# GNN and mixture-of-experts layer: node normalisation and gate logits moved into the closing visits of the attention stage

## The chip, the cores and the metric

The kernel runs on one core of a Trainium2 chip. The metric is device time of one execution in microseconds (us). A core has five engines with instruction streams of their own: TensorE (PE; its weight loads are listed as PEld), VectorE (DVE), ScalarE (ACT), GpSimd (POOL) and SyncE (SP). They meet only at semaphores, and 16 DMA engines serve all of them. "SPq", "POOLq" and the like are the queues that issue an engine's instructions.

## The reference

There are 6250 nodes with 256 features and 206,250 edges sorted by target node. The computation, cut to what matters:

```
h   = layernorm(x)                          # 6250 x 256
z   = h @ W                                 # 4 heads of 64
es, ed = (z * a_src).sum(-1), (z * a_dst).sum(-1)
e   = leaky_relu(es[src] + ed[dst])         # per edge and head
out = segment_sum(softmax_per_dst(e) * z[src], dst)
x   = x + out
hn  = layernorm(x)
logits = hn @ gate_w + gate_b               # 16 experts, the top 2 are taken
y   = hn + moe(hn)                          # 2 of 16 experts, hidden size 512
x   = x + layernorm(y) * gamma + beta
```

## The kernel before

Nodes stand in 49 tiles of 128. The program has five stages with a barrier of all engines between them: A (projection to z), B (attention), C (normalise, gate, sort the tokens to experts), D (experts), E (combine and store). The change touches B and C, and one load of A.

Stage B works in visits. 128 x 4 edges are a group, there are 403 groups, and a visit is one pair of a group and a tile of target nodes that the group touches: 403 - 1 + 49 = 451 visits, in order, written out without a loop (`written_out`, L90). A pass over all visits stands in a loop that runs once with these inputs. In step i each engine does, in the order in which its list stands (L776, L829, L861), the stages whose lag fits:

- POOL gathers the 512 rows of z of a group with four indirect DMAs into a slot of `ring` (L629 to L639). Before group g it waits until the messages of group g - 4 are made (`group_free`, `LEAD` = 4), although the ring has eight slots.
- SP relays each landed group to ACT (L580) and loads the target numbers of two groups at a time into `dst_bc`.
- ACT copies the source terms `es_edge` of visit i - 8 (L807), writes the target numbers of visit i - 9 (L796) and takes the exponent of visit i - 9 (L814, L816).
- DVE makes the one-hot matrix `ST` of visit i (L688), the argument of the exponent of visit i - 6 in four small steps (L702, L707, L713, and the clamp L720, which signals `b_arg`), adds visit i - 9 to the sums `acc` (L775), makes the one-hot `S` (L694) and the weighted messages (L761) of visit i - 7.
- PE multiplies `ST` of visit i with the node terms into `psE` (`destination`, L847) and then `S` with the messages of visit i - 7 into `psM` (`weigh`, L858).

`S`, `ST` and `msg` have eight buffers each (`SR`), and `S` and `ST` lie in the memory of `xs`, on top of 32 tiles of x. The results of two visits share a bank of `psE`: before an even visit v, `destination` waits for the clamp of visit v - 7, and `e_add` waits until both visits of its bank are written.

The number of a tile's last visit depends on the input, but tile t is surely closed after visit 402 + t. So work on closed tiles can be written only beside the last visits. Before, `settle` and `weight` (L729, L818) scale the sums of the first 36 tiles there, and add and take the statistics of the first 12. The pass ends with SP waiting for every semaphore, clearing 24 of them one by one (L620 to L622) and releasing the engines; a barrier follows, in which POOL drains.

Stage C then reloads x over `S` and `ST` (L923 to L925), scales the last 13 tiles on ACT (L979), and in a pipeline over 49 tiles adds the sums to x (L1105), takes statistics (L1062), inverts the deviation, normalises a tile (L1128), stores it to `norm_rows` for stage D (L932), transposes it on PE (L1008), copies it on ACT (L977), multiplies it with the gate (L1016) and keeps 16 logits per node (L1134). After the last logit, top-2 and the sorting of tokens begin on DVE (L1143). Beside this POOL makes an iota and masks (L939 to L946), and DVE some constants (`setup`, L1070), which wait for POOL only at the tenth tile.

Of the kernel before, what the change touches and what calls it, by code (L numbers as in the profile page):

```python
# [28 lines left out]
I32 = mybir.dt.int32  # L29
# [5 lines left out]
P = 128  # L35
G = 4
RING = 8
LEAD = 4
# [12 lines left out]
AHEAD = 6  # L51
ZR = 12
# [37 lines left out]
def written_out(count, unroll, stages):  # L90

    for i in range(count + max(lag for _, lag in stages)):
        for stage, lag in stages:
            v = i - lag
            if 0 <= v < count:
                stage(v, v % unroll, v // unroll)
# [7 lines left out]
def gnn_moe_kernel(nc, E, x, x_turned, src_cols, dst_cols, dst_flat, dst_last, W, a_src, a_dst, gate_w, gate_b, w1, b1, w2, b2, gamma, beta, out):  # L104
# [18 lines left out]
    KEPT = NT - 1 - 32  # L123
# [25 lines left out]
    with whole:  # L149
# [17 lines left out]
        acc = sb(attention, "acc", [P, NT, ROW])  # L167
        esed = sb(attention, "esed", [P, NT, 2 * HEADS])
# [7 lines left out]
        group_free = sb(graph, "group_free", [1, GROUPS + RING - LEAD], I32)  # L176
# [46 lines left out]
        with ExitStack() as ctx:  # L223
# [28 lines left out]
            def _(sp):  # L252
# [120 lines left out]
            def _(dve):  # L373
# [71 lines left out]
                def aside(t, s, r):  # L445
# [18 lines left out]
                    if t == TABLES + 6:  # L464
# [12 lines left out]
                        step(nc.vector.tensor_tensor(group_free[:, RING - 1:GROUPS + RING - LEAD], psA[2][0:1, 0:GROUPS - LEAD + 1],  # L477
                                                     iota_f[0:1, 0:GROUPS - LEAD + 1], ALU.add))
# [14 lines left out]
                dve.wait_ge(a_late, 16 * 3)  # L493
# [38 lines left out]
        b_vstep = sem("b_vstep")  # L532
        b_pstep = sem("b_pstep"); b_nodes = sem("b_nodes")
        b_landed = [sem(f"b_landed{i}") for i in range(RING)]
        b_group = sem("b_group"); 
        PAIRED, PAIRS = RING // 2, -(-GROUPS // 2)
        b_dst = [sem(f"b_dst{i}") for i in range(PAIRED)]; b_rows = sem("b_rows"); b_over = sem("b_over"); b_go = sem("b_go")
# [5 lines left out]
        SETTLED = 3 * PART  # L543
        CLOSED = VISITS - 1 - (NT - SETTLED)
        assert CLOSED >= 0 and CLOSED + 11 >= 2 * 8 + (VISITS - 2 * 8) // 8 * 8
        SH = 2 * HEADS
        PASS_STEPS = 8
        FIN_STEPS = 2 + BULK - 1
        SR = 8
        with ExitStack() as ctx:  # L550
# [5 lines left out]
            stats_b = decided[:, :, :].rearrange("p t h -> p (t h)")[:, 0:PART * 6].rearrange("p (t c) -> p t c", c=6)  # L556
# [4 lines left out]
            dst_bc = sb(ctx, "dst_bc", [P, RING, G * P], BF16)  # L561
            earg = sb(ctx, "earg", [P, 4, 3, G * HEADS])
            msg = sb(ctx, "msg", [P, SR, G, ROW])
            psE = [ps(ctx, f"psEb{i}") for i in range(SR // 2)]
            psM = [ps(ctx, f"psMb{i}") for i in range(2)]
            psP = [ps(ctx, f"psPb{i}") for i in range(2)]

            def dest_of(s):

                return psE[s // 2][:, (s % 2) * G * SH:(s % 2 + 1) * G * SH]  # L570
# [3 lines left out]
            def _(sp):  # L574
                npass = sp.value_load(npass_i[0:1, 0:1], min_val=1, max_val=PASSES_MAX)
                with sp.Fori(0, npass) as k:
# [12 lines left out]
                    def replace_pair(g, at):  # L589

                        done = sp.value_load(group_free[0:1, bass.ds(g + 1, 1)], min_val=1, max_val=VISITS)
# [11 lines left out]
                    for g in range(GROUPS):  # L603
# [4 lines left out]
                        if g % 2 and g // 2 + PAIRED < PAIRS:  # L608
                            replace_pair(g + RING - 1, g // 2 % PAIRED)
# [3 lines left out]
                    for done, total in ((b_group, GROUPS), (b_rows, PAIRS), (b_S, VISITS), (b_ST, VISITS), (b_dest, VISITS), (b_estep, 3 * VISITS),  # L613
                                        (b_arg, VISITS), (b_p, VISITS), (b_msg, VISITS + 1), (b_sum, VISITS), (b_acc, VISITS), (b_es, VISITS),
                                        (b_fstep, FIN_STEPS), (b_rden, 1), (b_scaled, SETTLED), (b_added, PART // BATCH), (b_stats, PART),
                                        (b_var, 1), (b_pstep, PASS_STEPS), (b_nodes, 1)):
# [918 lines left out]
```

## Time and profile before

| | |
|---|---|
| Median of 3 runs | 2792.49 us (2790.86 to 2793.21) |
| The profiled execution, own time | 2791.16 us |
| Its span | 2789.3 us |
| Busy share: PE, DVE, ACT, POOL | 81%, 61%, 24%, 66% |
| Mean granted TensorE clock | 0.821 |
| Stage A | 0 to 78 us |
| Stage B | 78 to 2147.7 us |
| Stage C | 2147.7 to 2300.6 us, its tile pipeline until 2228.9 us |
| Stages D and E | from 2300.6 us |

Times of rows count from the span's start. An engine that is busy all the time is not always the one that sets the pace: here the idle time before each instruction, and what ended it, tell more than the shares. A row of the timeline merges consecutive instructions of one group and gives their start, the time that they took together, and in brackets the idle time before them with its releaser. "issue" means that the engine waited for nothing that the profile shows. The granted clock is 0.5 at 1.2 GHz and 1.0 at 2.4 GHz.

### The profile page before, as it was taken

To read this page: it belongs to the slowest core of one execution; us is meant where nothing else is said; L and a number is where in the kernel's file an instruction comes from. 1 tells how busy PE (TensorE), PEld (TensorE's weight loads), DVE (VectorE), ACT (ScalarE), POOL (GpSimd) and SP (SyncE) were. 2 spreads that over 40 slices of the span, in tenths; PEclk is the share of its full clock that TensorE was granted. 3 is DMA by queue.
4 is the path that set the end of the run, shared out by engine and by line. 5 is a ranking of instruction groups with operands and counts; after the bars stand their busy time and mean duration, and the time that the engine had idled before them with its cause. 6 is when DMAs were issued, how large, how long until landed. Compare 5 with 4: busy or idle time off the path is not lost. (4 is left out here: it accounts for less than half of the span.)

```text
span 2789.3 us, 54969 instructions
## 1 busy us (share of the span) xinstructions
PE 2258.7 (81%) x10829; PEld 1890.7 (68%) x10830; DVE 1711.3 (61%) x4828; ACT 682.4 (24%) x2857; POOL 1849.1 (66%) x1949
## 2 busy tenths in 40 slices
PE   7688787877878788887888888777884848999997
PEld 5576666666666666666766666666663818999985
DVE  6666666666666666666666666666666674333336
ACT  4111111111111111111111111111115415555557
POOL 0677777777777777777777777777774025555547
PEclk9677888788787887888787788888877559999998
DMA  9444444445454444555454554444554207633328
GB/s 315 121 133 133 130 133 131 133 133 132 132 133 133 133 132 130 133 133 133 133 134 134 133 133 133 132 128 133 134 132 127 87 0 243 197 103 106 107 93 278
DMA packets 183503, 382.70 MB, mean 137 GB/s; under 512 B 38837, under 2 KB 86880, under 8 KB 182474
## 3 DMA queue, kind: packets, MB, share of 16 engines
q0 software_dynamic: 87744, 243.02, 32.6%
q1 hardware_dynamic: 79656, 122.51, 13.7%
q10 hardware_dynamic: 15842, 14.43, 2.0%
q8 instruction: 74, 1.21, 0.2%
q14 instruction: 187, 1.53, 0.2%
HBM read 345.87 MB, written 33.93 MB: 136 GB/s over the span
## 5 line engine op out<-in xcount | busy, mean ns | idle before, releaser
L636 POOL DMA_INDIRECT ring<-z_table,src_idx x1612 | 1556.4, 965 | 496.0 <-issue 458.1
L858 PE MATMUL psMb<-msg,xs 128*128 128x260 f32 x3608 | 1202.5, 491 | 255.4 <-DVE msg L761 253.5
L858 PEld LDWEIGHTS psMb<-msg,xs 128*128 128x128 f32 x3608 | 827.1, 241 | 432.4 <-DVE msg L761 284.0
L847 PEld LDWEIGHTS psEb<-nodes,xs 128*128 128x128 f32 x3608 | 550.0, 224 | 269.3 <-issue 238.2
L847 PE MATMUL psEb<-nodes,xs 128*128 x3608 | 522.7, 272 | 156.5 <-DVE xs L688 155.9
L761 DVE TENSOR_TENSOR msg<-ring,psPb 128x1024 f32<-128x1024 f32 x451 | 546.4, 1211 | 0.0
L807 ACT COPY es_edge<-ring 128x16 f32 x451 | 91.8, 204 | 1679.2 <-SPq L583 1642.6
L702 DVE TENSOR_TENSOR earg<-es_edge,psEb 128x16 f32<-128x16 f32 x451 | 76.1, 169 | 559.5 <-ACT es_edge L807 555.4
L694 DVE TENSOR_TENSOR xs<-iota_f,psPb 128x512 f32<-128x512 f32 x451 | 305.9, 678 | 0.1
L688 DVE TENSOR_SCALAR xs<-dst_bc,iota_p 128x512 f32 x451 | 229.9, 510 | 99.5 <-issue 95.2
L1275 POOL DMA_INDIRECT rows_sb<-norm_rows,src_sb x108 | 109.8, 1017 | 168.1 <-DVE src_sb L1352 149.7
L1307 PE MATMUL psHd<-xT,w_sb 128*128 128x128 f32 x1728 | 213.2, 277 | 0.0
L775 DVE TENSOR_TENSOR acc<-acc,psMb 128x260 f32 x451 | 188.1, 417 | 36.8 <-PE psMb L858 31.4
L1319 PE MATMUL psYd<-w_all,hid 128*128 x864 | 204.4, 380 | 0.3 <-ACT hid L1342 0.3
L1307 PEld LDWEIGHTS psHd<-xT,w_sb 128*128 128x128 f32 x1728 | 204.2, 194 | 0.1
L1363 DVE COPY xT<-psXd 128x256 f32<-128x256 f32 x108 | 45.9, 425 | 255.9 <-PE psXd L1297 255.9
L1319 PEld LDWEIGHTS psYd<-w_all,hid 128*128 128x128 f32 x864 | 156.1, 191 | 17.3 <-issue 0.5
L1330 ACT COPY w_sb<-w_all 128x1024 f32 x108 | 112.8, 1045 | 156.7 <-PE psHd L1307 96.6
L1282 POOL DMA_INDIRECT pair_rows<-y_sb,dst_sb x108 | 107.0, 991 | 45.5 <-issue 36.1
L1342 ACT ACTIVATE hid<-psHd,b1T 128x128 f32<-128x128 f32 x432 | 123.6, 368 | 34.1 <-issue 25.9
L796 ACT ACTIVATE psPb<-dst_col,visit_base 128x4 f32 x451 | 120.5, 267 | 1.4 <-issue 1.4
L814 ACT ACTIVATE msg<-earg 128x16 f32<-128x16 f32 x451 | 91.0, 202 | 54.2 <-DVE earg L720 49.5
(209 smaller groups left out, 1413.3 us busy)
## 6 DMA issues: line engine op xcount, KB each, us to landing
dst_bc<-dst_rows SPq DMA_DIRECT2D x202, 256.0 KB, 3.5
ring<-z_table,src_idx POOLq DMA_INDIRECT x1612
w_all<-in_L_ffn_w_dram SPq DMA_DIRECT2D x32, 512.0 KB
b_sb<-in_L_ffn_b_dram ACTq DMA_DIRECT2D x108, 128.0 KB, 3.1
got<-pair_rows SPq DMA_DIRECT2D x48, 256.0 KB, 4.2
xs<-in_x_dram SPq DMA_DIRECT2D x5, 1536.0 KB, 10.9
z_table<-z_out SPq DMA_DIRECT2D x49, 130.0 KB, 6.3
norm_rows<-xnc SPq DMA_DIRECT2D x49, 128.0 KB, 1.7
```

The costliest lines, as they stand in the source:

```text
L636: nc.gpsimd.indirect_dma_start(ring[:, s, c, :], None, z_table, bass.IndirectOffsetOnAxis(ap=at, axis=0)).then_inc(b_landed[s], 16)
L688: nc.vector.tensor_scalar(ST[:, s, :], dst_bc[:, bass.ds(slot, 1), :].rearrange("p o f -> p (o f)"), iota_p[:, 0:1], None, ALU.is_equal).t ...
L694: nc.vector.tensor_tensor(S[:, s, :, :], over(iota_f[:, 0:P].unsqueeze(1), [P, G, P]), over(psP[s % 2][:, G * HEADS:G * HEADS + G].unsquee ...
L761: nc.vector.tensor_tensor(msg[:, s, :, 0:D].rearrange("p g (h d) -> p g h d", h=HEADS), ring[:, bass.ds(slot, 1), :, 0:D].rearrange("p o g ...
L775: nc.vector.tensor_tensor(at, at, psM[s % 2][:, 0:ROW], ALU.add).then_inc(b_acc, 1)
L796: nc.scalar.activation(psP[s % 2][:, G * HEADS:G * HEADS + G], dst_col[:, bass.ds(group * G, G)], ACT.Identity, bias=visit_base[:, v:v + 1])
L847: last = nc.tensor.matmul(dest_of(s)[:, c * SH:(c + 1) * SH], ST[:, s, c * P:(c + 1) * P], nodes[:, bass.ds(tile, 1), :].rearrange("p o c ...
L858: last = nc.tensor.matmul(psM[s % 2][:, 0:ROW], S[:, s, c, :], msg[:, s, c, :], start=c == 0, stop=c == G - 1)
L1307: last = nc.tensor.matmul(psH[s % 2][:, f * P:(f + 1) * P], w1_sb[:, s % 2, c, f * P:(f + 1) * P], xT[:, s % 2, c, :], start=c == 0, stop= ...
L1319: last = nc.tensor.matmul(psY[s % 2][:, 0:D], hid[:, s % 2, f, :], w2_f, start=f == 0, stop=f == FC - 1)
L1330: nc.scalar.copy(w1_sb[:, s % 2, :, :].rearrange("p c f -> p (c f)"), w_all[:, bass.ds(e, 1), 0:KD * F].rearrange("p o f -> p (o f)")).the ...
L1342: last = nc.scalar.activation(hid[:, s % 2, f, :], psH[s % 2][:, f * P:(f + 1) * P], ACT.Relu, bias=b1T[:, bass.ds(e, 1), f:f + 1].rearran ...
```

## The change

Four things change together.

- Memory: `S` and `ST` become tensors of their own, so x stays in `xs`, and the reload in stage C goes. The ring falls from eight groups to four, with the same wait for group g - 4; `dst_bc` keeps eight (`ROWS`). `S`, `ST` and `msg` have four buffers (`MR`) instead of eight.
- Banks: four visits share one bank of `psE` (`BANKED` = 4), which leaves two banks for `psT` and `psL`. Before a visit v divisible by four, `destination` waits for the clamp of visit v - 5, which DVE makes in step v + 1; `e_add` waits until all four visits of its bank are written.
- The work: `finish` on DVE, ACT and PE takes over the whole per-tile pipeline of stage C. In batches of three tiles the denominators are inverted (DVE), the sums scaled (ACT), added to x and measured (DVE). Each six tiles the root is taken (ACT, between two exponents) and inverted. From step 426 on one tile per step is normalised (now on ACT), stored (issued by ACT), transposed (PE), copied (ACT), multiplied with the gate (PE) and its logits kept (DVE). `psT` and `psL` are single. The last batch is tiles 45 to 48; tile 48 is normalised in step 474, and the visits end in step 459. Stage C begins with the constants, a wait for POOL's iota and mask, and top-2.
- The turn of a pass: 35 semaphores with consecutive numbers are cleared by one instruction, and POOL drains right after its last gather.

```diff
-RING = 8
-LEAD = 4
+RING = 4
+ROWS = 8
+BANKED = 4
+                sp.dma_start(gate[:, :, :], gate_w.rearrange("(c p) e -> p c e", p=P)).then_inc(a_late, 16)
+        BATCHES = [range(t, t + BATCH) for t in range(0, NT - NT % BATCH - BATCH, BATCH)]
+        BATCHES.append(range(BATCHES[-1].stop, NT))
+        NB = len(BATCHES)
+        SPANS = [(n, n + 1) for n in range(0, NB - 2, 2)] + [(n,) for n in range(NB - 2, NB)]
+        SUMMED = AHEAD + 2 + MSG_TO_ACC
+        CLOSES = [FULL + tiles.stop - 1 + SUMMED for tiles in BATCHES]
+        WEIGHED = {CLOSES[n] + 2 + min(i, 2): [] for n in range(NB) for i in range(BATCH)}
...
+                NORMED[max([CLOSES[batches[-1]] + 9] + [at + 1 for at in NORMED])] = (t, p)
+        FINISH = max(NORMED) + 6
         SR = 8
+        MR = 4
-            S = xs[:, KEPT:KEPT + 2 * SR, :].rearrange("p (s o) c -> p s (o c)", o=2).rearrange("p s (g e) -> p s g e", g=G)
-            ST = xs[:, KEPT + 2 * SR:KEPT + 4 * SR, :].rearrange("p (s o) c -> p s (o c)", o=2)
+            S = sb(ctx, "S", [P, MR, G, P])
+            ST = sb(ctx, "ST", [P, MR, G * P])
-                    for done in (*b_dst, b_group, ...):
-                        sp.sem_clear(done)
+                    sp.sem_clear(range(b_pstep.num, b_saved[-1].num + 1))
-                        done = pool.value_load(group_free[0:1, bass.ds(g + RING - LEAD, 1)], min_val=0, max_val=VISITS)
+                        done = pool.value_load(group_free[0:1, bass.ds(g, 1)], min_val=0, max_val=VISITS)
+                    pool.drain()
-                        both = v + 2 - s % 2
-                        dve.wait_ge(b_dest, (min(both, VISITS) if isinstance(v, int) else both))
+                        dve.wait_ge(b_dest, min(v + BANKED - s % BANKED, VISITS))
@@ stage B, vector: closed batches (the last batch is scaled here as well), then spans, then one tile's logits
+                    def finish(i):
+                        for n, tiles in enumerate(BATCHES):
+                            if i == CLOSES[n]:
...
+                            if i == CLOSES[n] + 3:
+                                dve.wait_ge(b_scaled, tiles.stop)
+                                nc.vector.scalar_tensor_tensor(out=xs[:, at, :], in0=acc[:, at, 0:D], scalar=passes_left[:, 1:2], in1=xs[:, at, :],
+                                                               op0=ALU.mult, op1=ALU.add).then_inc(b_added, 1)
+                            if i == CLOSES[n] + 4:
...
+                        for p, batches in enumerate(SPANS):
+                            if i == CLOSES[batches[-1]] + 4:
+                                dve.wait_ge(b_stats, at.stop)
+                                bulk_rstd(fin_step, stats, at, b_var)
+                            if i == CLOSES[batches[-1]] + 6:
+                                dve.wait_ge(b_root, p + 1)
...
+                        if i - 3 in NORMED:
+                            dve.wait_ge(b_log_ps, t + 1)
+                            nc.vector.tensor_tensor(logits[:, t, :], psL[:, 0:EXPERTS], gate_row[:, :], ALU.add).then_inc(b_log, 1)
@@ stage B, scalar
+                    def finish(i):
...
+                            if i == CLOSES[batches[-1]] + 7:
+                                nc.scalar.activation(rstd[:, at], ln_tmp[:, 0, at], ACT.Sqrt, bias=eps_col[:, 0:1]).then_inc(b_root, 1)
+                        if i in NORMED:
+                            nc.scalar.activation(xn[:, t % XN, :], xs[:, t, :], ACT.Identity, bias=shift[:, t:t + 1], scale=rstd[:, t:t + 1]).then_inc(b_xn, 1)
+                        if i - 1 in NORMED:
+                            act.dma_start(norm_rows[t * P:(t + 1) * P, :], xn[:, t % XN, :]).then_inc(b_saved[t % XN], 16)
+                        if i - 2 in NORMED:
+                            act.wait_ge(b_xT_ps, t + 1)
+                            nc.scalar.copy(xnT[:, t % XN, :], psT[:, 0:D]).then_inc(b_xT, 1)
-                        if s % 2 == 0 and not early(v, SR):
-                            pe.wait_ge(b_arg, v - SR + 2)
+                        if s % BANKED == 0 and not early(v, SR):
+                            pe.wait_ge(b_arg, v - SR + BANKED)
@@ stage B, tensor
+                    def finish(i):
+
+                        if i - 1 in NORMED:
+                            t, _ = NORMED[i - 1]
+                            pe.wait_ge(b_xT, t + 1)
+                            if t:
+                                pe.wait_ge(b_log, t)
...
+                        if i + 1 in NORMED:
+                            t, _ = NORMED[i + 1]
+                            pe.wait_ge(b_xn, t + 1)
+                            if t:
+                                pe.wait_ge(b_xT, t)
...
@@ stage C, vector
+                step(nc.vector.tensor_copy(iota_h[:, :], iota_f[:, 0:P]))
+                step(nc.vector.tensor_scalar(tile_h[:, :], iota_f[:, 0:NT], 1.0, None, ALU.add))
+                step(nc.vector.memset(resets[:, :, :], 1.0))
+                step(nc.vector.memset(resets[:, :, 0:1], 0.0))
+                dve.wait_ge(c_iota, 2)
+                step(nc.vector.tensor_copy(reverse[:, :], reverse_i[:, :]))
```

## Rows read from the trace of the kernel before

**Rows 1.** Waits of the whole run: us in total, times, longest.
```profile
POOL ring L636 <- issue: 458.1, 1504, 0.3
```

**Rows 2.** The gather's line: duration min/median/max in ns, first and last start.
```profile
L636 POOL DMA_INDIRECT ring<-z_table,src_idx x1612: 942/946/3990, 80.7 to 2126.8; - x180
```

**Rows 3.** Stretches: length, busy time of each engine, granted clock, DMA share.
```profile
1937.00:2093.00 156.00, 129.24 (x555) 107.12 (x554) 101.42 (x274) 20.73 (x136) 118.53 (x124) 0.78 0.50 132
2149.60:2229.00 79.40, 61.81 (x295) 58.02 (x295) 51.37 (x183) 31.72 (x106) 0.66 (x4) 0.50 0.38 133
```

**Rows 4.** Timeline, the last accumulation and the first step of top-2.
```profile
2139.62 0.42 DVE L775 TENSOR_TENSOR acc<-acc,psMb 128x260 f32 x1 [1.89 <-PE psMb L858]
2228.91 0.97 DVE L1143 TENSOR_REDUCE top<-logits 128x49 f32<-128x784 f32 x1
```

**Rows 5.** Timeline, a group's first gather and the last message it waited for.
```profile
2116.95 1.21 DVE L761 TENSOR_TENSOR msg<-ring,psPb 128x1024 f32<-128x1024 f32 x1
...
2123.04 0.95 POOL L636 DMA_INDIRECT ring<-z_table,src_idx  x1 [0.30 <-issue]
```

**Rows 6.** Timeline, one step of DVE with no wait in it.
```profile
1013.30 1.21 DVE L761 TENSOR_TENSOR msg<-ring,psPb 128x1024 f32<-128x1024 f32 x1
...
1014.99 0.41 DVE L775 TENSOR_TENSOR acc<-acc,psMb 128x260 f32 x1
...
1016.00 0.16 DVE L720 TENSOR_SCALAR earg<-earg 128x16 f32<-128x16 f32 x1
```

**Rows 7.** Timeline, PE's two parts of a visit at either clock.
```profile
1006.36 3.63 PE L858 MATMUL psMb<-msg,xs 128*128 128x260 f32 x8 [1.16 <-DVE msg L761]
...
1014.56 2.02 PE L858 MATMUL psMb<-msg,xs 128*128 128x260 f32 x8
...
1016.42 0.95 PE L847 MATMUL psEb<-nodes,xs 128*128 x8
...
2101.20 1.72 PE L847 MATMUL psEb<-nodes,xs 128*128 x8
```

**Rows 8.** Timeline, DVE's addition to x and statistics beside a gather.
```profile
2113.40 1.01 DVE L741 SCALAR_TENSOR_TENSOR xs<-acc,passes_left,xs 128x768 f32<-128x768 f32 x1
2114.33 1.07 DVE L747 BATCH_NORM_STATS2 decided<-xs 128x6 f32<-128x256 f32 x3
...
2113.65 1.58 POOL L636 DMA_INDIRECT ring<-z_table,src_idx  x1 [0.30 <-DVE msg L761]
```

**Rows 9.** Timeline, ACT: scaling of three tiles, table load, root, copy.
```profile
2097.78 2.96 ACT L827 ACTIVATE acc<-acc,pass_tmp 128x64 f32<-128x64 f32 x12
2147.74 1.28 ACT L965 ACT_TABLE_LOAD   x1 [5.02 <-PEq L550]
2149.04 0.30 ACT L965 ACTIVATE rstd<-ln_tmp,eps_col 128x12 f32<-128x12 f32 x1
2218.97 0.37 ACT L977 COPY xnTc<-psTc 128x256 f32<-128x256 f32 x1 [0.80 <-PE psTc L1008]
```

**Rows 10.** Timeline, PE and the logits of two neighbouring tiles late in stage C.
```profile
2217.55 0.87 PE L1016 MATMUL psLc<-gate,xnTc 128*128 128x16 f32 x4
2218.26 0.67 PE L1008 MATMUL psTc<-ident,xnc 128*128 128x128 f32 x2
2218.72 0.87 PE L1016 MATMUL psLc<-gate,xnTc 128*128 128x16 f32 x4
```

**Rows 11.** Lines of the turn: duration min/median/max ns, first and last start.
```profile
L622 SPq EVENT_SEMAPHORE_RANGE_CLEAR  x24: 25/25/34, 2143.7 to 2145.0; - x24
L550 POOLq DRAIN  x1: 2354/2354/2354, 2145.1 to 2145.1; - x1
```

**Rows 12.** POOL after a change of its configuration: stage A, and stage C with the configuration's line.
```profile
65.84 0.39 POOL L370 PARTITION_ALL_REDUCE spread_all<-spread  x1 [6.26 <-issue]
L939 POOLq MODIFY_POOL_CONFIG  x2: 12/12/12, 2147.8 to 2147.9; - x2
2157.58 0.14 POOL L939 IOTA reverse_i<- 128x16 int32 x1 [29.84 <-issue]
```

More of the change, by code:

```diff
@@ L87, in pipeline, with written_out @@
                 stage(rounds * unroll + at, at % unroll, rounds + at // unroll)
-def written_out(count, unroll, stages):
-    for i in range(count + max(lag for _, lag in stages)):
+def written_out(count, unroll, stages, steps=0):
+    for i in range(max(steps, count + max(lag for _, lag in stages if lag is not None))):
         for stage, lag in stages:
+            if lag is None:
+                stage(i)
+                continue
             v = i - lag
@@ L122, in gnn_moe_kernel @@
     FULL_CHUNKS = E // P
-    KEPT = NT - 1 - 32
     DR, HEAD = 4, 12
@@ L167, in gnn_moe_kernel @@
         acc = sb(attention, "acc", [P, NT, ROW])
+        gate = sb(attention, "gate", [P, KD, EXPERTS])
+        logits = sb(attention, "logits", [P, NT, EXPERTS])
         esed = sb(attention, "esed", [P, NT, 2 * HEADS])
@@ L857, in weigh @@
                         for c in range(G):
-                            last = nc.tensor.matmul(psM[s % 2][:, 0:ROW], S[:, s, c, :], msg[:, s, c, :],
+                            last = nc.tensor.matmul(psM[s % 2][:, 0:ROW], S[:, s % MR, c, :], msg[:, s % MR, c, :],
                                                     start=c == 0, stop=c == G - 1)
                         last.then_inc(b_sum, 1)
-                    written_out(VISITS, SR, [(destination, 0), (weigh, AHEAD + 1)])
+                    def finish(i):
+                        if i - 1 in NORMED:
+                            t, _ = NORMED[i - 1]
+                            pe.wait_ge(b_xT, t + 1)
+                            if t:
+                                pe.wait_ge(b_log, t)
+                            for c in range(KD):
+                                last = nc.tensor.matmul(psL[:, 0:EXPERTS], xnT[:, t % XN, c * P:(c + 1) * P], gate[:, c, :],
+                                                        start=c == 0, stop=c == KD - 1)
+                            last.then_inc(b_log_ps, 1)
+                        if i + 1 in NORMED:
[3 more added lines that the diff above has]
+                                pe.wait_ge(b_xT, t)
+                            for c in range(KD):
+                                last = nc.tensor.transpose(psT[:, c * P:(c + 1) * P], xn[:, t % XN, c * P:(c + 1) * P], ident[:, :])
+                            last.then_inc(b_xT_ps, 1)
+                    written_out(VISITS, SR, [(destination, 0), (weigh, AHEAD + 1), (finish, None)], steps=FINISH)
                     pe.sem_inc(b_over, 1)
@@ L1132, in keep_logit @@
-                def keep_logit(t, s, r):
-                    dve.wait_ge(c_log_ps, t + 1)
-                    nc.vector.tensor_tensor(logits[:, bass.ds(t, 1), :].rearrange("p o e -> p (o e)"), psL[s % 2][:, 0:EXPERTS],
-                                            gate_row[:, :], ALU.add).then_inc(c_log, 1)
-                pipeline(dve, NT, PART, PART, [(add_sums, 0), (norm, 0), (next_part, 0), (setup, 0), (keep_logit, 3)], tail=PART + 1)
-                dve.wait_ge(c_log, NT)
+                step(nc.vector.tensor_copy(iota_h[:, :], iota_f[:, 0:P]))
```

300 lines of the change are left out of this document (94 added, 206 removed).

## The prediction

> **What bounds the kernel now.** I first asked the list of waits who sets the pace of stage B. POOL's 1612 gathers stand 0.3 us apart with no other reason than issue, and no gap is longer [rows 1]: it never waited for anything. They run from 80.7 to 2126.8 us [rows 2], so a group takes 2046/402.75 = 5.08 us and one of the 451 visits 4.54 us. DVE needs 2.78 us for a step in which nothing is late (from the end of one clamp at 1013.30 to the next at 1016.08) [rows 6]; in the last full stretch PE was busy 129.2 of 156 us, about 3.8 us per visit at a granted clock of 0.78, and ACT 20.7 [rows 3]. So B is POOL-bound, and work added to DVE, ACT or PE is free while their steps stay under 4.54 us. What the reader is to see next is that nothing covers the path after the last visit: from the end of the last accumulation (2139.62 + 0.42 = 2140.04) to the first reduction of top-2 (2228.91) 88.9 us pass [rows 4], and POOL does almost nothing in the tile pipeline (0.66 of 79.4 us) [rows 3]. This stretch is what the change works on. Stages A, D and E stay.
>
> **The 88.9 us that go.** The turn is 7.7 us (2140.04 to the root's table load at 2147.74 [rows 9]): ACT's remaining scaling, SP's waits, 24 clears from 2143.7 to 2145.0, then 2.35 us of POOL's drain [rows 11]. The rest, 81.2 us, is stage C up to top-2.
>
> **What comes in its place.** Five terms.
>
> *1. Steady stage B (about 360 groups).* The ring is neutral: before and after, group g waits for the messages of group g - 4; the index into `group_free` falls by four with the ring. The loads of `dst_bc` wait for the same visits. Four buffers of `S`, `ST` and `msg` are enough, since DVE has already waited for the accumulation of visit v - 2 when it makes `S` of v. The bank wait is different. Before every fourth visit PE now stands until DVE's clamp in step v + 1, one step later than ST allows, and behind `destination(v)` in its queue stands `weigh(v-7)`, whose sum DVE adds in step v + 2. From the end of a clamp to that accumulation DVE takes 1014.99 - 1013.30 = 1.7 us if nothing is late [rows 6], and up to 1.7 + (4.54 - 2.78) = 3.5 us when it waits for the gather. PE needs 0.95 + 2.02 = 3.0 us at the full clock and 1.72 + 3.63 = 5.4 us at half [rows 7]. So DVE is late by 0 to 1.9 us in the usual rhythm and by up to 3.7 us behind a group with two visits. What covers it: the last group's gather began at 2123.04 and its message had ended at 2118.16, 4.9 us before [rows 5], and DVE regains 1.8 us a visit. The cost lies between 0 and, with the full 3.7 us lost at each of 103 banks, 380 us; the nearest row is the 4.9 us of slack, so I take 3 us, for the few places where a double visit and a slow PE meet.
>
> *2. The closing steps 414 to 459.* DVE per batch of three tiles: three small ops for the denominators 0.6, the addition 1.01 and three statistics 1.07 [rows 8], half of a span's eight small ops and stepping 0.84, three logits 0.5: 4.0 us, or 1.34 per step. 2.78 + 1.34 = 4.1 us. ACT: 1.0 for scaling a tile (2.96 for three), about 0.4 for the normalisation and 0.37 for the copy [rows 9], some 0.3 of DMA issue, 0.6 of its own (20.7 of 156 us [rows 3]): 2.7 us. PE: 0.67 + 0.87, which overlap to 1.17 a tile at the lower clock (2218.72 - 2217.55) [rows 10], and about half at the full one; with 3.0 and 5.4 for the visit, 3.6 or 6.6 us. At a granted clock of 0.78, 56% of the time is at the full level, and PE's mean rate gives 1/(0.56/3.6 + 0.44/6.6) = 4.5 us. So DVE and ACT fit and PE is level with POOL. The bounds: 0, and 34 steps (426 to 459) at 6.6 - 4.54, 70 us. I take 8 us, near the mean clock's row: PE has no reserve left for a low stretch, but a PE that is always busy has fewer idle stretches.
>
> Two things more fall in here. The root sits between exponents: six roots in steps 424 to 454 need two table loads each, 2 x 1.28 + 0.30 [rows 9] = 2.9 us on ACT, of which the second load stands before an exponent that the message waits for. Two ACT steps hold 9.1 us and 5.4 + 2.9 = 8.3 are used: nothing on the path, up to 6 x 1.3 = 8 us if it slips. The addition to x reads two operands from SBUF, and a gather beside it took 1.58 instead of 0.95 us [rows 8]; the longest of the four such places. Fourteen additions fall before the last gather, four did before: ten more at 0 to 0.6 us each; I take 1.
>
> The Trainium skill speaks against these roots: its page "ScalarE: Activation LUTs", section "What ACT_TABLE_LOAD costs", gives some 1.28 us for a load and another 1.38 us of drain at every change of set. By the row the root starts 0.02 us after the load's end and the load is 1.28 us [rows 9], with no such drain; by the page each of the six pairs would take 2.8 us more, the two steps 11.1 of 9.1 us, and 6 x 2.0 = 12 us would be added.
>
> *3. The tail.* Tile t is normalised in step 426 + t, so tiles 34 to 48 come after the last visit, and three more steps until the last logit: 17 steps. `psT` and `psL` are single, so PE, ACT and DVE hand over within a tile; as long as that hides in PE's own 1.17 us [rows 10] this is 20 us. Beside it DVE must, from step 460, invert and scale the last four tiles (0.6 + 1.5), take statistics of tiles 42 to 44 (1.1), add the last four (1.3), measure them (1.45) and run two spans (3.3): 9.3 us in steps 460 to 466, while PE waits for `b_log` of the tile before. Some 2 us hide. 27 us; between 20 (all hidden) and 36 (1.17 + 0.37 + 0.2 of handing over per tile, 9 on top).
>
> *4. The turn.* SP's last wait to the clears 0.5, one clear, branch and barrier 0.8: 1.3 us; the drain's 2.35 us [rows 11] are paid beside the tail. If a second drain costs the same, 3.7.
>
> *5. Stage C before top-2.* The constants are some 1.4 us of DVE (two casts and two memsets of at most 784 elements). But DVE then waits for POOL's iota and mask. POOL set its configuration at 2147.8 and the iota began at 2157.58, 9.8 us later; in stage A another such instruction stood idle for 6.26 us [rows 12]. Before, the pipeline covered this; now nothing does. With the mask behind it DVE goes on 10.6 us after the stage's start. Between 1.5 (no such delay without the reload of x beside it) and 10.6; I take 10.6, from the same instruction.
>
> **Sum.** 3 + 8 + 1 + 27 + 1.3 + 10.6 = 50.9 us instead of 88.9: 38 us less. The load of `gate` in stage A is one more issue on SP before the first z is there: nothing. The profiled execution took 2791.2 us (its span 2789.3), so 2753.2 by its account; the median of before lies 1.3 us above that execution: 2754.5 us.
>
> **Rivals.**
> - *A: the closing is free and POOL quick.* With no reload beside it the iota comes after the 6.3 us of stage A's row, the closing costs 2 and the tail 23 us: 3 + 2 + 0 + 23 + 1.3 + 6.9 = 36 us, 53 less: 2740 us. For it: DVE and ACT fit. Against: POOL's delay ended long before DVE needed it, so no row shows what it hangs on.
> - *B: PE falls to the lower clock in the closing.* Transposes and 16-column products kept it at 0.50 through all of the tile pipeline [rows 3]. At 6.6 us per step the closing costs 45 to 70 us instead of 8: 2792 to 2817, say 2797 us. Against: the long products of the visits still run.
> - *C, the other side: the bank wait bounds stage B.* Place: `destination` of every fourth visit. If the stall lasts (PE idle before the boundary, thus at half clock behind it), DVE no longer regains it and POOL starts waiting. It decides from 35 to 38 us over 103 boundaries, 0.36 us each. At 0.8 us each, 83 us: 2754 + 80 = 2834 us. For it: 5.4 us against 3.5. Against: 4.9 us of slack, and 4 x 5.4 + 1.4 = 23 us per four visits only if the clock is low all the time, against 18.2; at the clock of 0.78 it is about 17.
> - *D: roots on the path*, by the page's rule as worked out above, as a mechanism: the exponent is late after each of six roots by 2.0 us. 2754 + 12 = 2766 us.
>
> **Chances.** My forecast 0.50 (own range 2745 to 2765), A 0.20, D 0.10, B 0.10, C 0.10. A measurement here can tell about 0.2% (5.6 us) from no change. Faster by more than that: forecast, A, D and a little of B, 0.82; within it 0.05 (B at 45 us); slower 0.13. The range 2733 to 2792 leaves out C, most of B, and a sliver below, about 2 in 10.
>
> **What would show it.** Right: gathers 0.3 us apart until about 2127 us with no wait for messages outside the closing; the last accumulation at 2147 to 2157 us; some 27 us to the last logit; one clear; a POOL drain of well under 1 us after it; DVE idle about 9 us before `reverse` with the iota as releaser. Wrong: DVE's accumulation waiting for PE in every fourth visit and POOL for DVE (C); a granted clock near 0.5 from about 1990 us (B); ACT behind each root (D); `reverse` without a wait (A). A median above 2792 would mean that a wait was added to the 451 visits; one below 2733, that the tail costs less than PE's own time per tile.

## The result, and the profile after

The changed kernel takes 2832.5 us (median of 4 runs, 2826.1 to 2843.6), the kernel before 2792.0 (2790.9 to 2793.2) on the same chip: a ratio of 1.0149, 95% interval [1.0132, 1.0166]. It is 40 us slower where 38 us less were forecast, and it lies within 2 us of rival C (2834). The profiled execution took 2826.1 us, its span is 2824.3.

The end of stage B has moved like this (us from the span's start, each the first gather of a group or the row named):

| | before | after | later by | forecast |
|---|---|---|---|---|
| group 358 gathered | 1900.1 | 1925.5 | 25.4 | 3 |
| group 402 gathered | 2123.0 | 2200.2 | 77.2 | 12 |
| last accumulation ends | 2140.0 | 2223.9 | 83.9 | 12 |
| from there to the last logits | | 29.3 | | 27 |
| turn of the pass | | 1.3 | | 1.3 |
| from there to top-2 | | 7.9 | | 10.6 |
| top-2 starts | 2228.9 | 2262.4 | 33.5 | -38 |

The last accumulation is 2140.0 before (2139.62 + 0.42) and 2223.9 after (2223.48 + 0.42). What was forecast of the tail, the turn and stage C came out within 3 us each. The whole error lies before the last accumulation: it comes 83.9 us later where 12 were forecast, 25.4 of them in the steady stage (3 forecast) and 58.5 behind it (9 forecast).

The waits of the changed kernel over the whole run (us in total, times, longest); POOL's first line answers to [rows 1]:

```profile
PE psEb L912 <- DVE earg L750: 472.2, 111, 8.1
POOL ring L666 <- issue: 456.6, 1475, 2.0
DVE acc L820 <- PE psMb L923: 296.3, 142, 4.5
```

The first line did not exist before: TensorE stands at the destination matmuls (L912) until VectorE's clamp (L750), 111 times, 4.3 us each. The visits 8, 12, and so on to 448 ask for a bank that was used before, which makes 111. This is the wait of the four-visit banks, at all of them. VectorE then waits for TensorE at its accumulation 142 times, 296.3 us in sum, where it was 38 times and 31.4 us before.

How much of it reaches POOL, which bounds the stage, is in POOL's waits of the steady stage (window 131 to 1925 us after, 131 to 1900 before):

```profile
POOL ring L666 <- issue: 396.7, 1289, 1.5
POOL ring L666 <- DVE msg L806: 57.5, 112, 3.4
```

```profile
POOL ring L636 <- issue: 397.5, 1305, 0.3
POOL ring L636 <- DVE msg L761: 28.9, 95, 0.3
```

454.2 us of idle time against 426.4: 27.8 more, which is about the steady stage's 25. The longest wait was 0.3 us and is 3.4. TensorE stood 406 us at 98 banks in that window, so only about a fifteenth of it reached POOL. The rest was hidden by the slack between the end of a message and the gather that asks for it.

One boundary in the middle of the run, TensorE and then VectorE of the changed kernel (columns as in [rows 6, 7]):

```profile
1014.74 1.87 PE L912 MATMUL psEb<-nodes,ST 128*128 x8 [5.37 <-DVE earg L750]
1016.47 3.81 PE L923 MATMUL psMb<-msg,S 128*128 128x260 f32 x8
1020.07 1.71 PE L912 MATMUL psEb<-nodes,ST 128*128 x8
1021.64 3.45 PE L923 MATMUL psMb<-msg,S 128*128 128x260 f32 x8
```

```profile
1014.33 0.17 DVE L750 TENSOR_SCALAR earg<-earg 128x16 f32<-128x16 f32 x1
1014.40 1.21 DVE L806 TENSOR_TENSOR msg<-ring,psPb 128x1024 f32<-128x1024 f32 x1
...
1020.58 0.43 DVE L820 TENSOR_TENSOR acc<-acc,psMb 128x260 f32 x1 [3.01 <-PE psMb L923]
1025.39 0.43 DVE L820 TENSOR_TENSOR acc<-acc,psMb 128x260 f32 x1 [1.90 <-PE psMb L923]
1028.24 0.41 DVE L820 TENSOR_TENSOR acc<-acc,psMb 128x260 f32 x1
1031.02 0.41 DVE L820 TENSOR_TENSOR acc<-acc,psMb 128x260 f32 x1
```

The clamp ends at 1014.50, the first matmul starts 0.24 us later, after 5.37 us of idleness. The two visits behind it then take 1.87 + 3.81 and 1.71 + 3.45 us, near the durations of the lower clock [rows 7]; the granted clock was 0.52 from 1014.7 to 1025.1 us and 1.00 from there to 1033. VectorE waited 3.01 and 1.90 us for their sums. In the next two steps it waits for nothing and accumulates 2.8 us apart: there it makes up for the delay before the next boundary.

In the closing the same wait meets the new work (changed kernel, all engines, lines left out):

```profile
2139.57 0.35 DVE L750 TENSOR_SCALAR earg<-earg 128x16 f32<-128x16 f32 x1
2139.65 1.21 DVE L806 TENSOR_TENSOR msg<-ring,psPb 128x1024 f32<-128x1024 f32 x1
2140.78 1.07 DVE L781 BATCH_NORM_STATS2 stats_b<-xs 128x6 f32<-128x256 f32 x3
...
2143.06 0.17 DVE L195 SCALAR_TENSOR_TENSOR ln_tmp<-ln_tmp 128x6 f32<-128x6 f32 x1
2143.14 0.17 DVE L796 TENSOR_TENSOR logits<-psLb,gate_row 128x16 f32<-128x16 f32 x1
...
2145.91 0.35 DVE L750 TENSOR_SCALAR earg<-earg 128x16 f32<-128x16 f32 x1
...
2146.51 1.87 PE L912 MATMUL psEb<-nodes,ST 128*128 x8 [8.15 <-DVE earg L750]
2148.24 3.36 PE L923 MATMUL psMb<-msg,S 128*128 128x260 f32 x8
2151.43 0.51 PE L935 MATMUL psLb<-gate,xnTb 128*128 128x16 f32 x4
2151.79 0.42 PE L944 MATMUL psTb<-ident,xnb 128*128 128x128 f32 x2
...
2152.25 0.37 ACT L893 COPY xnTb<-psTb 128x256 f32<-128x256 f32 x1 [8.18 <-PE psTb L944]
2153.09 0.20 ACT L851 COPY es_edge<-ring 128x16 f32 x1 [0.47 <-issue]
2153.33 0.17 DVE L732 TENSOR_TENSOR earg<-es_edge,psEb 128x16 f32<-128x16 f32 x1 [1.17 <-ACT es_edge L851]
```

Read it as a ring; it is one place, and that the others are like it is read from the sums below. TensorE waits 8.15 us for the clamp at 2145.91, which comes late because a batch's statistics and variance, 2.4 us from 2140.86 to 2143.23, stand before it in VectorE's list. The transposes of a tile stand behind that wait in TensorE's queue, ScalarE's copy waits 8.18 us for them, the next visit's `es_edge` stands behind the copy, and VectorE's first addition of the next step waits for `es_edge`. The waits of 1930 to 2224 us in sum:

```profile
ACT xnTb L893 <- PE psTb L944: 82.0, 21, 10.9
PE psEb L912 <- DVE earg L750: 62.0, 11, 8.1
POOL ring L666 <- DVE msg L806: 53.0, 22, 9.2
```

POOL's 53.0 us answer to the closing's 52 (77.2 - 25.4). The busy time by stretch, answering to [rows 3]:

```profile
1000.00:1200.00 200.00, 153.49 (x707) 131.88 (x707) 128.20 (x353) 27.76 (x176) 148.66 (x157) 0.81 0.49 131
1925.00:2200.00 275.00, 198.36 (x929) 170.63 (x930) 188.52 (x555) 112.63 (x437) 171.54 (x176) 0.76 0.43 120
2224.00:2254.50 30.50, 22.95 (x98) 18.99 (x98) 11.02 (x50) 12.67 (x32) 0.00 (x0) 0.53 0.18 63
```

No engine is full in the closing: TensorE 72%, VectorE 69%, POOL 62%, ScalarE 41% of 275 us. So no engine's load sets the pace; the waits above are a chain through all four.

The turn and stage C, answering to [rows 9, 11, 12]:

```profile
L670 POOLq DRAIN  x1: 8053/8053/8053, 2201.3 to 2201.3; - x1
L576 POOLq DRAIN  x1: 41/41/41, 2254.1 to 2254.1; - x1
L1003 POOLq MODIFY_POOL_CONFIG  x2: 11/11/11, 2254.5 to 2254.5; - x2
L1003 POOL IOTA reverse_i<- x1: 140/140/140, 2261.6 to 2261.6; 128x16 int32 x1
2262.16 0.17 DVE L1074 CAST reverse<-reverse_i 128x16 f32<-128x16 int32 x1 [6.15 <-POOL valid L1007]
2262.37 0.97 DVE L1078 TENSOR_REDUCE top<-logits 128x49 f32<-128x784 f32 x1
```

The first drain is issued while three gathers are still to run and ends at 2209.4, 4.5 us after the last of them (2203.91 + 0.95), beside the tail. The second costs 0.04 us, the iota comes 7.1 us behind the configuration, and VectorE stood 6.15 us for it, as forecast, somewhat shorter.

### The profile page after: what moved, and what is told of

Its sections match the earlier page's. It is cut to its first block and busy times, and to the rows that moved or that the text cites. A ratio compares the mean times of both kernels' runs of the same rounds, so it can differ in the third digit from the quotient of the medians.

```text
span 2824.3 us, 54568 instructions
## 1 busy us (share of the span) xinstructions
PE 2181.8 (77%) x10829; PEld 1874.5 (66%) x10830; DVE 1703.2 (60%) x4862; ACT 727.9 (26%) x2906; POOL 1847.7 (65%) x1949
## 3 DMA queue, kind: packets, MB, share of 16 engines
q8 instruction: 76, 1.25, 0.2%
## 5 line engine op out<-in xcount | busy, mean ns | idle before, releaser
L923 PE MATMUL psMb<-msg,S 128*128 128x260 f32 x3608 | 1152.2, 474 | 30.4 <-DVE msg L806 30.2
L912 PEld LDWEIGHTS psEb<-nodes,ST 128*128 128x128 f32 x3608 | 588.7, 237 | 587.4 <-issue 554.3
L912 PE MATMUL psEb<-nodes,ST 128*128 x3608 | 553.6, 281 | 503.9 <-DVE earg L750 472.2
L923 PEld LDWEIGHTS psMb<-msg,S 128*128 128x128 f32 x3608 | 807.4, 235 | 169.6 <-DVE msg L806 33.9
L820 DVE TENSOR_TENSOR acc<-acc,psMb 128x260 f32 x451 | 188.8, 419 | 302.1 <-PE psMb L923 296.3
L725 DVE TENSOR_TENSOR S<-iota_f,psPb 128x512 f32<-128x512 f32 x451 | 305.7, 678 | 0.3
L719 DVE TENSOR_SCALAR ST<-dst_bc,iota_p 128x512 f32 x451 | 226.9, 503 | 77.1 <-issue 74.2
L858 ACT ACTIVATE msg<-earg 128x16 f32<-128x16 f32 x451 | 92.3, 205 | 220.6 <-DVE earg L750 219.2
```

The costliest lines, as they stand in the source:

```text
L719: nc.vector.tensor_scalar(ST[:, s % MR, :], dst_bc[:, bass.ds(slot, 1), :].rearrange("p o f -> p (o f)"), iota_p[:, 0:1], None, ALU.is_equ ...
L725: nc.vector.tensor_tensor(S[:, s % MR, :, :], over(iota_f[:, 0:P].unsqueeze(1), [P, G, P]), over(psP[s % 2][:, G * HEADS:G * HEADS + G].un ...
L820: nc.vector.tensor_tensor(at, at, psM[s % 2][:, 0:ROW], ALU.add).then_inc(b_acc, 1)
L912: last = nc.tensor.matmul(dest_of(s)[:, c * SH:(c + 1) * SH], ST[:, s % MR, c * P:(c + 1) * P], nodes[:, bass.ds(tile, 1), :].rearrange("p ...
L923: last = nc.tensor.matmul(psM[s % 2][:, 0:ROW], S[:, s % MR, c, :], msg[:, s % MR, c, :], start=c == 0, stop=c == G - 1)
```

## The experiments

All experiments ran on three other chips, on which every kernel takes about a quarter longer (the kernel before 3454 to 3538 us); the last experiment looks at what differs. Neither the banks alone nor a shorter lead was timed on the first chip. A set is a group of kernels timed side by side on one chip. Sets 2, 3 and 5 ran on the same chip, and the kernel before still took 3538, 3461 and 3527 us there, so each ratio is to the kernel before in the same set, and sizes in us are best compared within a set. "Steady" is the first gather of group 8 to that of group 358, "closing" from there to group 402, in us, both from one profile each. They scatter: the closing of the lead of 5 was 310.0 to 316.6 us in four profiles, that of the changed kernel 342.1 and 317.1 in two, and a profiled execution lay up to 19 us off the median of its kernel.

| set | kernel | median us | ratio to before | steady | closing |
|---|---|---|---|---|---|
| 1 | before, four-visit banks | 3565.6 | 1.0327 [1.0258, 1.0396] | 2440.6 | 301.6 |
| 1 | before, ring and buffers of four | 3455.4 | 0.9994 [0.9960, 1.0027] | 2362.5 | 286.3 |
| 1 | changed, lead 5 | 3436.6 | 0.9956 [0.9934, 0.9978] | 2350.6 | 310.0 |
| 1 | changed, no root | 3521.0 | 1.0191 [1.0137, 1.0245] | 2451.4 | 317.9 |
| 2 | changed | 3628.2 | 1.0246 [1.0223, 1.0269] | 2492.5 | 342.1 |
| 2 | changed, lead 5 | 3524.1 | 0.9958 [0.9941, 0.9976] | 2419.5 | 313.5 |
| 2 | changed, lead 4 | 3523.8 | 0.9945 [0.9919, 0.9972] | 2435.3 | 311.5 |
| 2 | before, four-visit banks | 3648.9 | 1.0311 [1.0282, 1.0341] | 2504.8 | 305.3 |
| 3 | changed, lead 5 | 3437.7 | 0.9937 [0.9914, 0.9960] | 2348.5 | 316.6 |
| 3 | the same, later copies | 3428.7 | 0.9921 [0.9884, 0.9958] | 2341.4 | 310.0 |
| 3 | lead 5, no root | 3416.7 | 0.9866 [0.9820, 0.9912] | 2342.6 | 309.9 |
| 3 | lead 5, ramp on VectorE | 3436.0 | 0.9928 [0.9895, 0.9960] | 2347.7 | 315.5 |
| 4 | changed | 3550.0 | 1.0294 [1.0250, 1.0337] | 2435.1 | 317.1 |
| 4 | changed, lead 5 | 3434.7 | 0.9943 [0.9918, 0.9967] | 2367.1 | 314.1 |
| 4 | lead 5, ramp and later copies | 3427.5 | 0.9920 [0.9895, 0.9945] | 2353.0 | 306.6 |
| 4 | lead 5, bfloat16 | 3379.8 | 0.9794 [0.9743, 0.9845] | 2306.8 | 302.2 |
| 5 | before, lead 5 | 3530.2 | 1.0006 [0.9986, 1.0026] | 2412.6 | 300.3 |
| 5 | before, banks and lead 5 | 3537.1 | 1.0029 [1.0011, 1.0048] | 2421.6 | 301.8 |

**The banks alone**, in the kernel before:

```diff
-            psE = [ps(ctx, f"psEb{i}") for i in range(SR // 2)]
+            psE = [ps(ctx, f"psEb{i}") for i in range(SR // 4)]
-                        both = v + 2 - s % 2
+                        both = v + 4 - s % 4
-                        if s % 2 == 0 and not early(v, SR):
-                            pe.wait_ge(b_arg, v - SR + 2)
+                        if s % 4 == 0 and not early(v, SR):
+                            pe.wait_ge(b_arg, v - SR + 4)
```

> The kernel before with one part of the change alone: four visits share a bank of psE (two banks instead of four). Theory 1, the bank wait costs stage B its steady loss: the first gather of group 358 starts at about 1925 us (before 1900, after 1925), POOL waits for messages, and the time is 2792 + 25 to 30 = 2817 to 2822 us. Rival 1, the loss comes from the smaller ring or from four buffers of S, ST and msg: group 358 at 1900 us and 2792 us. The rows to see are PE's wait for the clamp and DVE's accumulation waiting for PE, each some 100 times.

> The kernel before with nothing but the four-visit banks. If the bank wait alone makes the steady stage longer: group 358 is gathered 20 to 30 us later than in the kernel before and the whole takes 25 to 35 us more, ratio 1.009 to 1.013. If it needs the short ring or the closing steps as well: under 5 us, ratio under 1.002.

3.3 and 3.1% slower, more than the whole change costs. On these chips the banks are enough to make the loss. They cost more there than the first chip's 25 us: the steady stage is 78 us longer than with the ring of four in the same set (2440.6 - 2362.5). Why it is three times as much is open.

**The ring alone**, in the kernel before: `RING = 4`, eight rows of `dst_bc`, four buffers of `S`, `ST` and `msg`, the index into `group_free` lowered by four.

> The kernel before with the other part alone: a ring of four groups, four buffers of S, ST and msg, pairs in the banks as before, x reloaded as before. Theory 1: no difference, 2792 us within 4, group 358 at 1900 us. Rival 1: the steady loss is here, 2815 us or more.

No difference that the measurement can tell. The short ring and the four buffers are neutral here, as the prediction had it.

**One visit of lead less**, in the changed kernel, which moves the clamp that opens a bank from step v + 1 to step v:

```diff
-AHEAD = 6
+AHEAD = 5
```

> The changed kernel with AHEAD = 5 instead of 6: with four visits to a bank, destination then waits for a clamp that DVE makes in its own step v and no longer in step v + 1. Nothing else of the change is undone. Theory 1: the steady loss goes (group 358 at 1900 to 1905 us instead of 1925), and of the 52 us lost in the closing 44 groups more than half, because the transposes stand in PE's queue behind the same wait: 2755 to 2785 us. Rival 1 (buffers) and rival 2 (table loads for the root): 2832 us within 10.

> The changed kernel unchanged, timed beside the others of this call so that they can be compared with it on one chip. Both theories: a ratio to the kernel before of 1.015 if this chip is like the first; if stage B is again longer by the stalls that the last four runs showed, 1.00 to 1.02.

> The changed kernel with one visit of lead less (AHEAD 6 to 5), so that the destination matmuls that open a bank of four wait for the clamp of the step that runs beside them instead of the step after. If the wait for the bank costs the steady stage its 25 us and a part of the closing: 25 to 45 us less than the changed kernel, ratio to the kernel before 1.000 to 1.006, group 358 gathered by about 1903 us of the span instead of 1925. If the four-group ring costs the steady stage: no change from the changed kernel, ratio 1.015.

> The changed kernel with a lead of 5 visits again, as the base of the three runs beside it. Ratio to the kernel before 0.994 to 0.998 if the chip is like those of the last eight runs, 0.998 to 1.006 if it is like the first; in both cases the closing 44 groups take 20 to 30 us more than the 286 us of the kernel before with a ring of four.

> The changed kernel unchanged, as the base of this call. Ratio to the kernel before 1.015 where TensorE's matmuls are not held back, 1.02 to 1.03 where they are, as in the last run of it (1.0246).

> The changed kernel with a lead of 5 visits. If the wait for the bank is what the changed kernel loses by, on any chip: at least 1.5% under the changed kernel of this call, steady stage as in the kernel before. Where TensorE is not held back the ratio to before is then 0.998 to 1.004; where it is, 0.994 to 0.996 as three times before.

Side by side the lead of 5 takes 104 and 115 us less than the changed kernel, 2.9 and 3.3%, and it is 0.4 to 0.6% under the kernel before in all four sets. A lead of 4 brings nothing more:

> The changed kernel with two visits of lead less (AHEAD 4): the destination matmuls that open a bank wait for a clamp that stands one step back in VectorE's list. If at a lead of 5 the wait for the bank still costs something, this is 5 to 15 us under it; if it is gone at 5, the two are alike, or this one is up to 10 us longer since the additions to a visit's edge logits then meet destination matmuls issued one step before.

**The control for the lead**: the kernel before with `AHEAD = 5`, alone and with the banks.

> The kernel before with nothing but a lead of 5 visits instead of 6; its banks hold two visits. It is the control for the lead: if the lead of 5 wins only by taking the wait for the four-visit bank away, this is the kernel before within 0.2%. If a shorter lead is worth something by itself, say by buffers that come free earlier, it is up to 1% faster, and that much of the difference between the changed kernel at leads of 6 and 5 is not the bank's.

> The kernel before with four-visit banks and a lead of 5. If the bank costs only by the clamp that stands one step late, the 3.1 to 3.3% that the banks alone cost are gone to within 0.4%. If four-visit banks cost also by the additions that wait for a whole bank's matmuls, 1 to 2% stay.

The lead alone is worth nothing (1.0006), and with it the banks cost 0.29% instead of 3.1 to 3.3%. So the lead of 5 works by taking most of the bank's wait away. TensorE's waits at the destination matmuls between 145 and 2560 us say the same, first with the banks alone (second profile of that kernel), then with the lead alone, then with both:

```profile
PE psEb L847 <- DVE earg L720: 723.7, 79, 15.1
```

```profile
PE psEb L847 <- issue: 131.6, 87, 3.4
PE psEb L847 <- DVE xs L688: 5.1, 8, 1.2
```

```profile
PE psEb L847 <- DVE earg L720: 200.3, 24, 12.1
```

24 waits are left, but they no longer reach POOL. Its waits for messages, in the same order, from the first groups until each kernel's group 358:

```profile
POOL ring L636 <- DVE msg L761: 763.9, 202, 13.3
POOL ring L636 <- DVE msg L761: 659.8, 142, 9.4
POOL ring L636 <- DVE msg L761: 655.3, 141, 8.9
```

The 655 us that are left in both kernels with the lead of 5 are not the bank's; the last experiment is about them.

**The roots.** `ACT.Sqrt` becomes `ACT.Identity`, so that ScalarE loads no second table; the square root is left out, in the changed kernel and in its lead of 5.

> The changed kernel with the function of the root's activation in the visits replaced by Identity, so that no table load stands between the exponents; the square root is left out of the node normalisation. Rival 2, the closing's loss is the twelve table loads on ACT: the closing 44 groups fall from 275 to 245 us or less and the time to 2800 us. Theory 1: they hide behind ACT's waits for PE, at most 8 us less, 2824 to 2832 us.

> Lead of 5, and the roots of the variances replaced by an Identity of the same shape, so that ScalarE loads no other table (it leaves the square root out). If the roots with their table loads and the wait for them stretch the closing, as rival D says: 10 to 20 us less than the lead of 5 alone. If they are hidden: the same within 3 us.

The first had no unchanged neighbour in its set and only shows that most of the loss stays without roots (1.0191). The second took 21 us less than the lead of 5. In the profiles 6.7 us of the difference lie in the closing and 6 in the steady stage, where no root is; from top-2 to the end it took 550.9 instead of 564.6 us. Without the root the logits are others, so other tokens go to other experts, and the last 13.7 us are probably no price of the roots; no run shows it. The closing of 309.9 us is no shorter than one of the lead of 5 with its roots (310.0), so no price of the roots in the closing is shown.

**The copies one step later** (`i - 2` to `i - 3` for the copy, and one step more for logit matmul and addition):

> Lead of 5, and in the closing ScalarE copies the transposed tile one of its steps later, TensorE's logit matmuls and VectorE's addition follow one step later. If the closing is stretched by ScalarE standing at its copy for transposes that lie behind a step's matmuls in TensorE's queue: 8 to 20 us less than the lead of 5 alone. If the roots or the mere quantity of work stretch it: the same within 3 us, or up to 1.4 us more for one more step in the tail.

9 us by the medians, but the means differ by 6.5 us with a standard error of 4.3, and the closing of 310.0 us is the one that the lead of 5 had in set 1. The tail takes 30.1 instead of 29.3 us. So the chain through ScalarE's copy is seen in the rows, and that moving the copy shortens the closing is not shown; a gain over some 15 us is ruled out.

**The ramp on VectorE**:

```diff
-                dve.wait_ge(c_iota, 2)
-                step(nc.vector.tensor_copy(reverse[:, :], reverse_i[:, :]))
+                step(nc.vector.tensor_scalar(reverse[:, :], iota_f[:, 0:EXPERTS], -1.0, float(EXPERTS), ALU.mult, ALU.add))
```

> Lead of 5, and in stage C VectorE makes the reversed ramp of the experts from the ramp it has, and waits for GpSimd only after the top two: 6 to 8 us less than the lead of 5 alone, the first reduction of the top two within 2 us of the last logits instead of 9. If GpSimd's work ends last anyway: no change.

From the last logits to top-2 it took 3.0 instead of 9.2 us in the profiles; the medians differ by 1.7 us, and the runs of either kernel scatter over 13 us and more, so a gain of 6 us is neither confirmed nor contradicted.

**All three together**:

> Lead of 5, the reversed ramp on VectorE and the later copies of the closing together. If the three gains add: 10 to 18 us under the lead of 5 alone (9 from the copies, 6 at the start of stage C), ratio to before 0.990 to 0.993 where TensorE is held back, 0.988 to 0.996 where it is not. If the closing is bound by something else: within 5 us of the lead of 5.

3427.5 us, 0.8% under the kernel before and 3.5% under the changed one: it beats both on that chip. Against the lead of 5 it gains 7 us by the medians, less than the sum expected.

**What slows these chips.** In the profiles of them VectorE stands idle for 5 to 12 us again and again, mostly 15 to 28 us apart, which it did nowhere on the first chip in stage B of the kernel before (no idle stretch over 5 us). TensorE began single matmuls of one visit after 1.2 to 2.6 us of idleness each in such an episode of the lead of 5, so I suspected TensorE's own load and made `S` and `msg` bfloat16 (it leaves the precision of the weighted sums out):

> Lead of 5, with the weighing matmuls' two operands in bfloat16 instead of float32, so that they take a quarter of the passes (it leaves the precision of the weighted sums out). It is for the long stretches, 9 us in every 27, in which this chip's TensorE began one matmul in 1.2 to 2.6 us: if these come from TensorE's own load, they are gone, and stage B goes at the pace of GpSimd's gathers, 1260 us for 252 groups or about 2750 us in all, however slow the kernel before is on this chip. If they come from elsewhere, from the transfers or from instructions that arrive late: still 9 us in 27, over 3300 us.

The suspicion failed as a full explanation: 3379.8 us, not 2750. The load did fall (from 1000 to 1200 us TensorE was busy 93 us instead of 129 in the lead of 5 of the same set, at a granted clock of 0.50 instead of 0.72), and so did the idle stretches of VectorE of 5 us and more between 131 and 2600 us: 62 with 505 us in sum, instead of 106 with 876. Whether the load plays a part in them is open. One episode of that kernel, lines left out:

```profile
207.53 0.95 POOL L666 DMA_INDIRECT ring<-z_table,src_idx  x1 [0.30 <-issue]
209.21 0.20 ACT L851 COPY es_edge<-ring 128x16 f32 x1 [4.71 <-issue]
210.63 0.27 ACT L840 ACTIVATE psPb<-dst_col,visit_base 128x4 f32 x1 [1.21 <-issue]
212.53 0.95 POOL L666 DMA_INDIRECT ring<-z_table,src_idx  x1 [0.30 <-issue]
217.92 0.42 DVE L820 TENSOR_TENSOR acc<-acc,psMb 128x260 f32 x1 [12.06 <-remote]
220.29 1.05 PE L923 MATMUL psMb<-msg,S 128*128 128x260 bf16 x4 [12.32 <-DVE msg L806]
```

VectorE, ScalarE and TensorE all stand, with light matmuls too, while POOL's gathers go on 1.25 us apart until 213.78; then POOL too stands, 9.21 us, for a message of VectorE. Single instructions keep their durations (a gather 0.95, a message 1.22 us). What holds them is open. In 12 of the first 15 idle stretches of the lead of 5 (set 3), and in 78 of its 117, no transfer of instructions runs, so late code is not a likely cause of most.

## Why the prediction was wrong

**The step that failed** is term 1, "the nearest row is the 4.9 us of slack, so I take 3 us". The mechanism was written down right (clamp of step v + 1, `weigh` behind `destination`), the bounds 0 to 380 us held, and the value in them was badly chosen. Two things were wrong in it. The delay was taken as an exception of a double visit with a slow clock; the waits show it at all 111 boundaries with 4.3 us each. And the slack was taken as one row late in the run, with VectorE gaining 1.8 us a visit; in fact, at the boundary shown, TensorE, having stood, does its next two visits at about the lower clock's durations (10.8 us in two steps of 4.54), and VectorE can regain nothing in them, only in the two steps behind. Most of it is made up before the next boundary; what is not came to 25 us instead of 3. Its size on the first chip rests on these waits; the isolation by runs is from the other chips.

**Term 2** was summed engine by engine (4.1, 2.7 and 4.5 us a step against 4.54) and gave 9 us instead of 52 up to the last group's gather. No load was above what it allowed: TensorE's share was 72%, nothing was full. What it missed, by the rows of the closing, is order: statistics in front of the clamp that opens a bank, transposes behind the bank's wait, a copy before the next `es_edge`. How the 52 us divide on the first chip is open. Elsewhere the bank's part of the closing was 28.6 us in one set (342.1 - 313.5) and 3.0 in another (317.1 - 314.1). The closing steps themselves are the rest: 310.0 - 286.3 = 24 us against the ring of four in one set, and 313.5 - 300.3 = 13 between two sets of one chip. Which link of the chain costs them is open.

**Rival C** had the right place and, at 2834, the right time, but not its division. It put 83 us into the steady stage; 25 came there, and 58 behind it, where the bank's part is open. That its number fits within 2 us is luck: it had the last accumulation 92 us later (80 + 12) and 83.9 came, and the median of the changed kernel lies 6 us above the profiled execution, which makes up for most of the difference. **Rival D** did not come on the first chip: in the whole profile of the changed kernel no wait is put down to an exponent (L858, L860), which is where D had its place, and 1.9 us in sum to a root (L876). On the other chips the roots' price is lost in the scatter of the profiles. The table loads were as in [rows 9]:

```profile
2154.70 1.28 ACT L876 ACT_TABLE_LOAD   x1
2155.99 0.30 ACT L876 ACTIVATE rstd<-ln_tmp,eps_col 128x6 f32<-128x6 f32 x1
...
2157.31 1.28 ACT L858 ACT_TABLE_LOAD   x1
2158.61 0.22 ACT L858 ACTIVATE msg<-earg 128x16 f32<-128x16 f32 x1
```

Both users start 0.01 to 0.02 us behind the load, and both loads within 0.02 us of the instruction before them. The Trainium skill ("ScalarE: Activation LUTs", "What ACT_TABLE_LOAD costs") adds 1.38 us of drain at a change of set; these rows don't agree. **Rival B** did not come: the granted clock was 0.76 in the closing against 0.78 before [rows 3]. **Rival A** had the closing free, and the iota 7.1 us behind the configuration lies at its end of that term.

The upper bound of the tail was added up wrongly: 17 x 1.74 + 9 is 38.6 us, not 36; the 29.3 measured lie inside either.

**Right**: the ring is neutral (0.9994); tail 29.3 for 27; turn 1.3; no price of a second drain (0.04 us); stage C 7.9 for 10.6. These saved what was said: 88.9 - 38.5 = 50 us behind the last accumulation.

**The chances.** C and B had 0.20 together and the range ended at 2792. A cost bounded by 0 and 380 us had been carried into the sum as 3, and into the range as a few us; with the bounds kept, the range had to reach past 2830.

## What to carry to other kernels

When buffers are merged, find for each new wait the step in which the releasing instruction stands, on the releasing engine's list: a wait released one step later than it is asked for comes at every boundary. The lead can repair it: here one visit of lead less removed a loss of 3%. Work added beside a full pipeline is to be looked at for what stands behind it in each in-order queue, before the loads are summed; and a single row of slack is no allowance for a stall that comes at every boundary.

## What the runs showed that I had not expected

- The same program took 2792 us on one chip and 3454 to 3538 on three others, with episodes of 5 to 12 us in which three engines stood while POOL went on until it lacked a message. Ratios between kernels kept their sign: the changed kernel 1.015 there, 1.025 and 1.029 here.
- Before, the POOL drain began 17 us after the end of the last gather (2126.79 + 0.95) and still took 2.35 us [rows 11]. After, the first drain ended 4.5 us behind the last gather, and a second one, 45 us later, took 0.04. Whether the first drain or the longer time made the second cheap is open.
- From POOL's configuration to its first iota 7.1 us passed without the reload of x beside it, 9.8 with it [rows 12].
- The weighing matmuls of a visit took 1.05 us in bfloat16 (granted clock 0.50 from 1000 to 1200 us of that run), 3.6 in float32 at the lower clock [rows 7].
